# Latent attention in a four-layer gated model: another way to its first score

## The reference

```python
def _rmsnorm(x, g):
    return x * jax.lax.rsqrt(jnp.mean(x * x, axis=-1, keepdims=True) + EPS) * g

def _mla(h, Wq, Wdkv, Wuk, Wuv, Wo):
    q = (h @ Wq).reshape(B, S, HEADS, hd)
    c = h @ Wdkv
    k = (c @ Wuk).reshape(B, S, HEADS, hd)
    v = (c @ Wuv).reshape(B, S, HEADS, hd)
    scores = jnp.einsum('bqhd,bkhd->bhqk', q, k) / jnp.sqrt(jnp.asarray(hd, h.dtype))
    scores = jnp.where(causal, scores, -1e9)
    a = jax.nn.softmax(scores, axis=-1)
    return jnp.einsum('bhqk,bkhd->bqhd', a, v).reshape(B, S, D) @ Wo
```

## Time and profile before

| | before |
|---|---|
| median of 3 runs | 1207.25 us (1205.1 to 1209.43) |
| the profiled execution | 1215.4 us |
| its span, first to last instruction | 1213.6 us |
| PE busy | 1001.9 us (83%) |
| DVE busy | 830.8 us (68%) |
| ACT busy | 521.4 us (43%) |
| POOL busy | 484.7 us (40%) |
| mean granted TensorE clock | 0.893 of full |

### The profile page before, as it was taken

One profiled execution on the slowest core, in us unless ns is written; L12 is line 12 of the kernel. 1 busy time (PEld: TensorE's weight loads), 2 busy tenths in 40 slices (PEclk: granted clock), 3 DMA queues, 4 the chain that ended last, 5 costly groups with the idle time before them and its releaser, 6 DMA issues.

```text
span 1213.6 us, 20585 instructions
## 1 busy us (share of the span) xinstructions
PE 1001.9 (83%) x6811; PEld 722.2 (60%) x6811; DVE 830.8 (68%) x2125; ACT 521.4 (43%) x1266; POOL 484.7 (40%) x433
## 2 busy tenths in 40 slices
PE   4798795677776989985998589989989999569977
PEld 2577633556666888963777333333356776347774
DVE  5699488499967667666999477667523333769972
ACT  2455251245422544563444237666733333135532
POOL 3244254246524556401555876574530000314430
PEclk8899796589977999997999959899988999589999
DMA  8200000000011111130000121222020000000001
GB/s 304 103 1 1 1 1 0 1 1 1 1 30 31 41 38 41 32 110 34 1 0 1 43 88 60 82 73 57 21 88 1 0 0 0 1 1 1 1 1 35
DMA packets 22964, 40.21 MB, mean 33 GB/s; under 512 B 6272, under 2 KB 17792, under 8 KB 22240
## 3 DMA queue, kind: packets, MB, share of 16 engines
q1 hardware_dynamic: 20384, 33.99, 8.5%
q0 software_dynamic: 2496, 5.16, 1.6%
HBM read 31.31 MB, written 7.82 MB: 32 GB/s over the span
## 4 chain that ended last, share of the span: by engine, by line
PE 49%; issue 20%; DVE 15%; POOL 10%; ACT 3%; DMA 1%; SPq 0%; DVEq 0%; POOLq 0%; ACTq 0%
PE ps L800 6%; PE ps L752 5%; POOL att L1410 5%; PE ps L742 4%; PE ps L716 4%; PE ps L961 4%; PE ps L933 3%; PE ps L812 3%; PE ps L945 3%; DVE mx L1680 2%; DVE rs L1694 2%; PE ps L534 2%; PE ps L598 1%; DVE stats L1577 1%; PE ps L699 1%
## 5 line engine op out<-in xcount | busy, mean ns | idle before, releaser
L1410 POOL TENSOR_TENSOR att<-att,ri 128x1232 f32<-128x1232 f32 x64 | 177.1, 2768 | 221.4 <-DVE ri L1700 221.4
L716 PE MATMUL ps<-VW,PT 128*128 128x128 f32 (+3 forms) x1280 | 159.3, 280 | 29.9 <-DVE x L1712 28.2
L716 PEld LDWEIGHTS ps<-VW,PT 128*128 128x128 f32 (+1 forms) x1280 | 149.9, 193 | 48.9 <-DVE x L1712 44.3
L1139 ACT ACTIVATE PT<-ps 128x512 f32<-128x512 f32 x128 | 69.8, 595 | 127.5 <-PE ps L699 127.5
L1131 ACT ACTIVATE att<-att 128x1232 f32<-128x1232 f32 x64 | 79.0, 1234 | 53.0 <-DVE att L1687 52.1
L699 PE MATMUL ps<-W,att 128*128 128x128 f32 (+1 forms) x640 | 84.3, 280 | 10.1 <-POOL att L1410 10.1
L1694 DVE TENSOR_REDUCE rs<-att 128x16 f32<-128x1232 f32 x64 | 91.2, 1425 | 0.0
L1809 DVE SCALAR_TENSOR_TENSOR U<-ps,w_c,U 128x128 f32 x128 | 36.0, 344 | 76.7 <-PE ps L752 76.7
L800 PE MATMUL ps<-PT,att 128*128 128x128 f32 x624 | 79.4, 282 | 10.2 <-issue 10.2
L752 PEld LDWEIGHTS ps<-U,att 128*128 128x128 f32 x512 | 67.4, 194 | 33.3 <-issue 31.1
L2053 DVE CUSTOM_DVE_ANT_0 C<-ps,cmaskb 128x512 bf16<-128x512 f32 (+1 forms) x128 | 71.1, 555 | 20.0 <-PE ps L933 16.6
(11 more groups left out here) (332 smaller groups left out, 2216.0 us busy)
## 6 DMA issues: line engine op xcount, KB each, us to landing
U<-in_ffn SPq DMA_DIRECT2D x1, 6176.0 KB, 23.9
U<-split SPq DMA_DIRECT2D x144, 32.0 KB
W<-split SPq DMA_DIRECT2D x144, 32.0 KB
W<-in_packed SPq DMA_DIRECT2D x1, 2162.5 KB, 22.4
U<-in_ffn SPq DMA_DIRECT2D x1, 2060.0 KB, 8.3
U<-in_moe SPq DMA_DIRECT2D x1, 2048.0 KB, 8.4
split<-VBD SPq DMA_DIRECT2D x4, 384.0 KB, 3.3
split<-W SPq DMA_DIRECT2D x4, 384.0 KB, 2.6
```

The source lines that it names most:

```text
L716: q = mm(attended(s, t), PT[0:m, t.slot(2), c, :], batch(VW, t.group)[0:m, c * D:(c + 1) * D], start=(c == 0), stop=(c == NC - 1))
L1410: tt(p, p, over_keys(ri[:, t.slot(2), :]), ALU.mult).then_inc(probs, 1)
```

## The change

It does five things. The key projection of batch 0 and its copy move from batch 1 to batch 0 on PE and ACT, with a wait for that batch's latent. The split of batch 0's keys moves from POOL to DVE, in norm_y's place between batches 1 and 2, which is written out. The key transfers of quads 0 and 1 move from SP's queue to ACT's, behind ACT's part of the latents. POOL takes each group of four roots in one instruction of 16 columns, its exponent a broadcast. PE gets 12 more turns of keep_warm between its wait for the latents and the first score.

```diff
--- before.py
+++ after.py
@@ -77,6 +77,8 @@
 
 WARM = {F1: 10, MLA: 18, MOE: 10, F3: 10}
 WARM_FOLD = 4
+EARLY_WARM = 12
+BY_ACT = 2
 EARLY = 3
 UNIT0 = 2
 
@@ -433,6 +435,16 @@
 
             return READS[name, n]
 
+        def stack(eng, side, n):
+
+
+            b, c = divmod(n, 4)
+            for i in range(PIECES):
+                for j in range(PIECES):
+                    at = HD * (PIECES * i + j)
+                    src = split2[side, b, (i, j)[side], 32 * c:32 * c + 32, :].rearrange("(d g) n -> d g n", g=WAYS)
+                    eng.dma_start((keys, queries)[side][at:at + HD, n % HOLD, :, :], src).then_inc(stacked[n % HOLD], 16)
+
         def probabilities(n, g):
 
             return homes[4 * (n % 2) + g]
@@ -485,27 +497,20 @@
                 sp.wait_ge(done, b + 1)
                 sp.dma_start(split2[side, b].rearrange("i p n -> p i n"), pieces).then_inc(out_done, 16)
 
-            def stack(side, n):
-
-
-                b, c = divmod(n, 4)
-                sp.wait_ge((k_spilled, q_spilled)[side], 16 * (b + 1))
-                for i in range(PIECES):
-                    for j in range(PIECES):
-                        at = HD * (PIECES * i + j)
-                        src = split2[side, b, (i, j)[side], 32 * c:32 * c + 32, :].rearrange("(d g) n -> d g n", g=WAYS)
-                        sp.dma_start((keys, queries)[side][at:at + HD, n % HOLD, :, :], src)\
-                            .then_inc(stacked[n % HOLD], 16)
-
             spill(1, 0)
             spill(0, 0)
+
+            def stack_of(side, n):
+                sp.wait_ge((k_spilled, q_spilled)[side], 16 * (n // 4 + 1))
+                stack(sp, side, n)
             for n in range(QUADS):
                 if n < HOLD:
                     sp.wait_ge(rows_zero, 2 * (n + 1))
                 else:
                     sp.wait_ge(kq_ps, WAYS * TB * (n - HOLD + 1))
-                stack(1, n)
-                stack(0, n)
+                stack_of(1, n)
+                if n >= BY_ACT:
+                    stack_of(0, n)
                 if n % 4 == 3 and n // 4 + 1 < B:
                     spill(0, n // 4 + 1)
                     spill(1, n // 4 + 1)
@@ -881,12 +886,13 @@
                 if b == 0:
                     pe.wait_ge(ld["mla"], 16)
                     mm(ps[:, 4, :], w_q, FT[:, cols(0)], start=True, stop=True).then_inc(first_ps, 1)
-                elif b == 1:
+                    pe.wait_ge(mla_sb, 1)
                     mm(ps[:, 5, :], w_uk, c_s[0:LAT, cols(0)], start=True, stop=True).then_inc(first_ps, 1)
             prepare(MLA, latents)
             pe.wait_ge(mla_sb, B)
             pe.wait_ge(k_flat, 1)
             pe.wait_ge(q_flat, 1)
+            keep_warm(EARLY_WARM)
 
             def beside(name, n):
 
@@ -1264,9 +1270,12 @@
                 if b == 0:
                     act.wait_ge(first_ps, 1)
                     go(q_rest, ps[:, 4, :], ACT.Copy, scale=HD ** -0.5).then_inc(q_flat, 1)
-                elif b == 1:
                     act.wait_ge(first_ps, 2)
                     go(k_rest, ps[:, 5, :], ACT.Copy).then_inc(k_flat, 1)
+            for n in range(BY_ACT):
+                act.wait_ge(k_spilled, 16)
+                act.wait_ge(rows_zero, 2 * (n + 1))
+                stack(act, 0, n)
             act.wait_ge(ones_set, 4)
 
             def beside(name, n):
@@ -1459,9 +1468,11 @@
             roots(X2)
             cross(X2)
             starts(pool, MLA)
-            roots(MLA)
-            for b in range(B):
-                root(ROUND0[MLA] + B + b, b, msq, rrms)
+            every = minus_half[:, 0:1].to_broadcast([P, NT])
+            pool.wait_ge(s_ve, ROUND0[MLA] + B)
+            tt(rstd[:, :], ve[:, :], every, ALU.pow).then_inc(s_rstd, B)
+            pool.wait_ge(s_ve, ROUND0[MLA] + 2 * B)
+            tt(rrms[:, :], msq[:, :], every, ALU.pow).then_inc(s_rstd, B)
             pool.wait_ge(ld["mla"], 16)
 
             def fill(r):
@@ -1493,7 +1504,6 @@
                     t.then_inc(chain, 1)
                     pool.wait_ge(chain, 3 * b + op + 1)
             split(1, 0, range(4))
-            split(0, 0, range(4))
             for r in range(1, HOLD):
                 fill(r)
             for held in held_at:
@@ -2033,7 +2043,17 @@
             for b in range(B):
                 normed(n0 + b, None, rows_of(x, b), rows_of(y, b), b)
             dve.wait_ge(s_xn, TB * (n0 + B))
-            norm_y(MLA, n0 + B, rrms)
+            for b in range(B):
+                normed(n0 + B + b, TURN0[MLA] + b, rows_of(y, b), xn_of(TURN0[MLA] + b), b, rms=rrms)
+                if b == 1:
+                    dve.wait_ge(k_flat, 1)
+                    v.tensor_copy(k_pieces[:, 0, :], k_rest).then_inc(k_chain, 1)
+                    dve.wait_ge(k_chain, 1)
+                    tt(k_rest, k_rest, k_pieces[:, 0, :], ALU.subtract).then_inc(k_chain, 1)
+                    dve.wait_ge(k_chain, 2)
+                    v.tensor_copy(k_pieces[:, 1, :], k_rest).then_inc(k_chain, 1)
+                    dve.wait_ge(k_chain, 3)
+                    tt(k_pieces[:, 2, :], k_rest, k_pieces[:, 1, :], ALU.subtract).then_inc(k_split, 1)
 
 
             v.memset(visible[:, 0:S - P], 0.0).then_inc(mask_set, 1)
```

## The result

| | before | after |
|---|---|---|
| median (range, runs) | 1207.25 us (1205.1 to 1210.65, 5) | 1217.57 us (1215.07 to 1224.03, 5) |
| ratio of after to before | | 1.009, 95% interval 1.0067 to 1.0112 |
| profiled execution | 1215.4 us, span 1213.6 | 1215.07 us, span 1213.3 |
| start of the last write of cross-attention 2 | 665.48 | 655.38 |
| from there to the first score of the latent attention, **X** | 34.2 us | 45.6 us |

The change makes the kernel 0.9% slower, some 10 us. The two profiled spans are equal by accident: the routed stage of layer 1 took 124.8 us (380.3 to 505.1) in the profiled execution of before and 115.3 us in that of after, in code that the change doesn't touch. So the two traces are compared from a common event inside them, the last write of x ahead of the stage.

What follows compares the result with a forecast made beforehand. Bound by a string of handovers from POOL's roots to PE's first score, no engine full. First score T0+24+4.4+8.6, +16.0 us; less 1.0 returned, net +15.0: median 1222, own range 1218 to 1227, 8-in-10 range down to 1206.

Steps and rivals of the forecast that it cites:

- before 702: First score of the latent attention: a start before 702 us would sink the forecast, which put it near 716.
- The 1230 for the profiled execution: Whole profiled run: the old one's 0.7% above its median was to carry over, giving 1230 against a median of 1222.
- T0 unchanged: End of batch 0's second norm: first root in one instruction taken as 2.2 us, done within 0.3 us of before.
- The hold: Norms of batches 2 and 3 on DVE: one instruction passes per POOL instruction, 14.4 us for eight, batch 3 normed at T0+24.
- Rival (d): Norms held half as long, two DVE instructions passing per POOL instruction: -7 on the forecast, 1215 us; chance 0.10.
- Tail and warming: From batch 3's norm to the first score: 4.4 us to the latents' copy, then 8.6 us of warming matmuls.
- Transfers on ACT's queue: Behind batch 3's copy: nine key issues and the landing take 4.9 us, hidden by the 8.6 us of warming.
- Returned: Start of scoring: full clock shortens the first matmul and side products by 1.0 us (range 0 to 3), then falls again soon.

Runs made afterwards that it cites:

- e5: Kernel before with only the key transfers of quads 0 and 1 issued by ACT's queue: X 35.8 us, ratio to before 1.0013 (0.9992 to 1.0035).
- e7: Kernel before with only 12 more warmings (96 matmuls) ahead of the first score: X 35.0 us, ratio to before 1.0015 (1.0001 to 1.003).
- e3: Kernel after without the 96 warming matmuls: X 44.7 us, ratio to before 1.0087 (1.0064 to 1.0111).
- e8: Kernel after with the key transfers of quads 0 and 1 back on SP's queue, warming kept: X 45.6 us, ratio to before 1.0079.
- e9: Kernel after with the key transfers back on SP's queue and without the 96 warming matmuls: X 38.0 us, ratio to before 1.0051.
- e12: Kernel after without added warming, key transfers on SP's queue, POOL's fills 1 to 3 waiting for batch 3's norm: X 34.4 us, ratio to before 0.9996.
- e2: Kernel after with POOL waiting for batch 3's norm before fills 1 to 3: X 43.5 us, ratio to before 1.0061.
- e1: Kernel after with DVE's key split behind batch 3's norm instead of batch 1's: X 41.7 us, ratio to before 1.0036.
- e4: Kernel before with only the two sets of four roots taken by one instruction each: X 36.1 us, ratio to before 1.003 (1.0015 to 1.0046).
- e6: Kernel before with only the key part: projection at batch 0, split on DVE behind batch 1's norm: X 40.2 us, ratio to before 1.0021.
- e11: Kernel before with queries' and keys' projections earlier, key split on DVE behind all norms, fills waiting, 160 instead of 144 warm matmuls: X 32.9 us, ratio 0.9969.

## Why the prediction was right, and where it was off

The direction and the mechanism were right: slower, because DVE's wait for the keys puts two norms behind it into POOL's fills. 1222 was forecast and 1217.57 measured, inside the range, 4.4 us less than the forecast; X grew by 11.4 us instead of 16.0. The first score at 701.02 is not the sign against the forecast that "before 702" was meant to be: the last write of cross-attention 2 stands 10.1 us earlier in this trace, so on the old scale the score is at 711.1. The 1230 for the profiled execution was wrong (1215.07): the 8 us by which the old one lay above its median did not carry over. By its steps, T0 being the end of batch 0's second norm (669.14 after):

- **T0 unchanged.** It is 13.8 us after the last write's start, against 13.2. The first root took 2.90 us, not 2.2, inside the bounds of 1.0 and 4.1. One thing I had not seen: the fill for quad 0 moved from beside the second norm to beside the first, so that the sixteen first-norm instructions took 7.30 instead of 4.19 and the four of the second norm 0.87 instead of 4.05. The sum is the same, and hid it.
- **Clock in the projections.** A step that is missing from the prediction. PE's idle time ahead of batch 0's turn grew from 1.71 to 2.42 us and the clock fell behind it, so that the keys were flat at T0+7.0 instead of T0+5.4, and the key split ended at T0+11.1 instead of T0+9 to 10. That the roots bring this about is not shown: e5 and e7 have it in part with the old ones.
- **The hold, the mis-sized term.** "One DVE instruction passes per POOL instruction" was too strict. The eight took 8.7 us over five POOL instructions, where 14.4 us were forecast. These 5.7 us are the largest error of the sum; against them T0 was 0.5 us and the start of the eight 1.4 us later, and the warming took about 1 us less, 4.6 us in all. Batch 3 was normed at T0+19.7, not T0+24. As the five POOL instructions ended, two, one, two, one and two of the eight ended too: two with each memset, one with each cast. Here is one beside the cast of 681.20, then the two beside the memset of 683.09, and last the two of the kernel before beside its memset of 674.76:

```profile
681.32 1.90 DVE L1610 TENSOR_SCALAR xn_s<-U,rrms 128x128 f32<-128x128 f32 x1
```

```profile
683.14 1.90 DVE L1610 TENSOR_SCALAR xn_s<-U,rrms 128x128 f32<-128x128 f32 x1
683.34 1.77 DVE L1610 TENSOR_SCALAR PT<-U,rrms 128x128 f32<-128x128 f32 x1
```

```profile
674.67 2.03 DVE L1600 TENSOR_SCALAR xn_s<-U,rrms 128x128 f32<-128x128 f32 x2
```

So the four that had taken 4.05 us beside two POOL instructions already showed it: two with the memset, one with the cast, the last one free. I extended the rate of the cast to all. Rival (d) had the better rate: two passing per POOL instruction gave 1215; 1.6 did pass, and the result lies between it and the forecast.

- **Tail and warming.** 4.6 us from the last norm to the latents' copy (4.4 forecast), 7.69 us of warming (8.6).
- **Transfers on ACT's queue, "4.9, hidden by the warming".** They were hidden, at the 7.4 us of e3 instead of 4.9. It follows, and the prediction did not say it, that the warming on the path is hidden just as well by them: e3, e8 and e9 show that neither of the two is to blame alone.
- **Returned.** 1.0 was forecast, and the 1.5 us between the two traces are no proof of it, since the stretch varies by more than that with and without warming. That the clock would fall again soon was right: it fell 3.9 us into scoring. By the Trainium skill (TensorE: Matmul & The Clock Gate, "Why this matters for your kernels") continuous work brings the full clock and short gaps keep it. Here the scores began at full clock and lost it after 3.9 us with gaps of 0.65 us at most, and 14.02 us of work in the next 15.10 did not bring it back; in e7 it was lost within 2 us. So the rows decide against that rule for this stretch.

The 11.4 us, then: the latents' last copy starts 12.2 us later, of which 3.8 us exceed the old first score (25.2 + 12.2 + 0.6 against 34.2), and 7.6 us of warming and transfers come behind it, where before the first score needed nothing more. e9 has the first part alone (X 38.0), e12 removes it too (34.4). Of the latents' 12.2 us the gate on the fills takes back 4.3 (e2, e12); the other 7.9 are DVE's wait for the keys, the later turns on PE and the half clock, not told apart here, and e12 shows that they alone cost nothing clear of the noise, as PE used to wait 9.00 us for the transfers. The hold pushes the latents past that cover. It needs the wait to do so: with the wait moved behind the norms (e1) the latents are as early as without the hold, 32.7 against 33.1.

What stays open: single traces and ratios differ by some microseconds, and X before may be a short one (34.2, where e5 and e7 have 35.8 and 35.0 with nothing changed ahead of the transfers). e4's 1.9 us of X are 0.16% and its ratio says 0.15 to 0.46%; e6 goes the other way. Whether the half clock in the projections befalls every execution of a kernel was not tried; in e7, with the old roots and 1.36 us of idle, a projection of 2.08 shows that it can happen in the kernel before too.

## What to carry to other kernels

Before work is moved to another engine, look at what stands behind it in that engine's order and at what the relieved engine will do in the time that it gains: here the relieved POOL ran ahead with fills that nobody needed yet and slowed the one engine that everyone waited for. One gate that holds them back takes 4.3 us off (e2), and with the two other costs gone nothing is left of the loss (e12). Two costs in parallel hide each other, so taking one out shows nothing (e3, e8); they must be taken out together (e9). And compare traces from a common event, not by their spans.

## What the runs showed of the hardware

- DVE instructions of 128x128 beside back-to-back POOL instructions of 1.9 us came out at one per 1.1 us, and at one per 0.22 with POOL silent (e2). POOL's memsets hold them as well as its casts; two passed per memset and one per cast (after, e3, e6, e8, e9). The Trainium skill (SBUF — State Buffer, "SBUF: two separate sides") tells of the exclusive lock; the rows of memsets, casts and of the multiplications of the earlier trace rows agree and add the rate. POOL's power instructions held nothing: in the kernel before, the sixteen first norms took 4.19 us beside these, 0.26 us each:

```profile
670.62 4.18 POOL L1377 TENSOR_TENSOR rrms<-msq,minus_half 128x4 f32<-128x4 f32 x4 [0.78 <-DVE msq L2032]
```

- A power instruction on POOL of 128x4 takes 1.03 us, one of 128x16 2.90 to 3.05: sixteen columns in one instruction cost less than four instructions of four (3.94), but the one can begin only when the last batch's variance is there, and ended 0.6 us later after the write (4.95 against 4.37).
- TensorE's clock stayed at 0.50 through 15.10 us in which it was 14.02 us busy with scores, and rose from 0.50 to 1.00 within 4.5 us of identity matmuls.
- The query spill came to rest 2.5 to 2.7 us after its issue in after and most experiments, 4.0 us in e4 and 4.6 us in e11 and before; nothing in these runs tells why.
